# Small stores every two steps, and folds that run five gathers behind, in a graph kernel's gather stage

## What is computed

```python
hw = jnp.einsum('ni,rio->rno', h, weight)          # 8 relations + self
msg = hw[rel, src] + bias[rel]                     # one row of 128 floats per edge
agg = jax.ops.segment_max(msg, dst, num_segments=n)
...
msg = h_rel[etype, src]                            # layer 2, twice
agg = jax.ops.segment_sum(msg, dst, num_segments=h.shape[0])
...
agg = jax.ops.segment_sum(t[src] * norm, dst, ...) # layer 3, four times
```

## Time and profile before

| | us |
|---|---|
| median of 3 runs | 3251.54 (3245.12 to 3256.81) |
| the profiled execution | 3260.87 |
| its span, first to last instruction | 3259.1 |
| the stage's first and last gather (L823), starts | 279.9 and 1423.8 |
| POOL busy in the gathers L823 | 906.2 |
| DVE waiting for gathered data | 367.2 |

### The profile page before, as it was taken

The page is one execution under the profiler, slowest core; times in us unless marked ns, Lnnn a source line. Parts: engine busy times, 40 slices in busy tenths (PEclk is TensorE's granted clock), DMA queues, the critical chain, the costliest instruction groups (busy, mean ns, idle before and its releaser), DMA issues. The chain is left out here.

```text
span 3259.1 us, 35088 instructions
## 1 busy us (share of the span) xinstructions
PE 2356.9 (72%) x12626; PEld 1177.6 (36%) x12626; DVE 1342.1 (41%) x2638; ACT 863.4 (26%) x1563; POOL 979.7 (30%) x870
## 2 busy tenths in 40 slices
PE   0583555555555555554699999998999999659995
PEld 0121111111111111122445555554555555347773
DVE  2617666666666666654210000002000000247675
ACT  1233656566665565642200000000000000210000
POOL 1314777777777777760000000000000000000000
PEclk9976667765666676666899999998999999769997
DMA  2431444454444444433143333315333333120000
GB/s 69 162 131 70 175 167 173 166 183 159 172 166 168 172 160 168 158 142 135 58 176 139 141 142 141 141 61 189 139 129 140 139 141 121 65 77 1 2 1 22
DMA packets 98038, 412.25 MB, mean 126 GB/s; under 512 B 20059, under 2 KB 43680, under 8 KB 79020
## 3 DMA queue, kind: packets, MB, share of 16 engines
q1 hardware_dynamic: 55398, 343.29, 28.0%
q0 software_dynamic: 27312, 56.42, 5.8%
q10 hardware_dynamic: 15126, 9.99, 1.0%
HBM read 252.08 MB, written 163.93 MB: 128 GB/s over the span
## 5 line engine op out<-in xcount | busy, mean ns | idle before, releaser
L1410 PE MATMUL ps_out<-arena,cut 128*128 128x512 fp8e4 x4900 | 1074.5, 380 | 3.0 <-DVE cut L1053 3.0
L823 POOL DMA_INDIRECT arena<-table_rel,key_rel x784 | 906.2, 1156 | 294.3 <-issue 228.3
L879 PE MATMUL ps_out<-arena 128*128 128x400 f16 x1568 | 531.1, 465 | 502.3 <-DVE arena L852 408.3
L903 ACT ACTIVATE arena<-ps_out 128x800 fp8e4<-128x800 f32 x784 | 607.8, 836 | 423.3 <-PE ps_out L879 420.5
L1410 PEld LDWEIGHTS ps_out<-arena,cut 128*128 128x128 f16 x4900 | 479.7, 98 | 567.2 <-issue 5.2
L835 DVE SCALAR_TENSOR_TENSOR arena<-arena,keep_max 128x128 f32<-128x128 f32 x784 | 272.3, 347 | 374.0 <-DMA arena<-table_rel,key_rel 367.2
L879 PEld LDWEIGHTS ps_out<-arena 128*128 128x128 f16 x1568 | 122.6, 112 | 814.7 <-DVE arena L852 434.8
L1378 ACT ACTIVATE tT<-ps_t 128x128 f32<-128x128 f32 x50 | 13.8, 277 | 1121.9 <-PE ps_t L1400 1121.9
L1093 PE MATMUL ps_out<-arena,cut 128*128 128x384 fp8e4 (+1 forms) x1500 | 214.8, 305 | 81.1 <-DVE cut L1053 53.2
L1362 DVE TENSOR_SCALAR CS<-ps_out,unit 128x512 f32<-128x512 f32 x49 | 36.7, 748 | 491.1 <-PE ps_out L1410 491.1
L1362 DVE TENSOR_SCALAR CS<-ps_out 128x512 f32<-128x512 f32 x49 | 33.8, 691 | 493.1 <-PE ps_out L1410 493.1
(11 more groups left out here) (252 smaller groups left out, 1423.4 us busy)
## 6 DMA issues: line engine op xcount, KB each, us to landing
arena<-adjacency SPq DMA_DIRECT2D x98, 1600.0 KB, 6.7
adjacency<-arena SPq DMA_DIRECT2D x49, 1600.0 KB, 5.6
running_rows<-arena SPq DMA_DIRECT2D x56, 896.0 KB
arena<-adjacency_plain SPq DMA_DIRECT2D x50, 400.0 KB, 7.9
table_rel<-arena SPq DMA_DIRECT2D x25, 512.0 KB
arena<-table_rel,key_rel POOLq DMA_INDIRECT x784, 3.0
adjacency_plain<-adj SPq DMA_DIRECT2D x25, 400.0 KB, 6.7
edge_rows<-edge_dst ACTq DMA_DIRECT2D x1, 3125.5 KB
```

The source lines that it names most:

```text
L823: e.indirect_dma_start(message(t), None, table, bass.IndirectOffsetOnAxis(key[:, t:t + 1], 0)).then_inc(s_msg[t % both], 16)
L879: last = e.matmul(g.ps_out[:, u % 2, q * 512:q * 512 + KW], g.hot_low[:, b % 2, k, :, q], g.hot_spot[:, b % 2, k, :, q], start=True, stop= ...
L903: e.activation(g.half[h % 2].rearrange("p (a w x) -> p a w x", a=NT, x=R * WIN)[:, :, at:at + 2, :], g.ps_out[:, u % 2, 0:1024].rearrange( ...
L1410: last = e.matmul(g.ps_out[:, h, 0:512], g.cut[:, a, part, :], adj[:, a, :], start=a + part == 0, stop=a + part == NT)
```

## The change

It has two parts. The stores go out in pieces, at most one of each kind for every two steps: the running maxima two rows at a time (128 KB, 1 KB per partition), a half tile of the adjacency in five pieces (320 KB, 2560 bytes per partition) at steps 6, 8, 10, 12 and 14 behind its completion, a plain tile in three pieces (128, 128 and 144 KB) from 16 steps behind its completion on. And the fold of step t waits until `s_begun` stands at t + 6 instead of t + 3: the gather of step t + 5 is about to be issued, where before it was that of t + 2. The counts in the waits on the store semaphores follow the number of pieces. Nothing is changed in what POOL, PE and ACT issue, nor in the order of DVE's work.

```diff
@@ -55,6 +55,8 @@
+BEHIND = 6
+ROWS, PARTS, THIRDS = 2, 5, ((0, 1024), (1024, 2048), (2048, 3200))
@@ -827,9 +829,9 @@
             def step(t):
                 e.wait_ge(s_msg[t % both], 16 * (t // both + 1))
-                e.wait_ge(s_begun, min(t + 3, STEPS))
+                e.wait_ge(s_begun, min(t + BEHIND, STEPS))
                 if t % HALF == 0 and t >= both:
-                    e.wait_ge(s_out[t // HALF % 2], 16 * (t // both))
+                    e.wait_ge(s_out[t // HALF % 2], 16 * (HALF // ROWS) * (t // both))
@@ -888,7 +890,7 @@
                 if at == 0 and 2 <= m < NT - 1:
-                    e.wait_ge(s_one[m % 2], 16 * (m // 2))
+                    e.wait_ge(s_one[m % 2], 16 * len(THIRDS) * (m // 2))
@@ -898,7 +900,7 @@
                     if at == 0 and h >= 2:
-                        e.wait_ge(s_sto[h % 2], 16 * (h // 2))
+                        e.wait_ge(s_sto[h % 2], 16 * PARTS * (h // 2))
@@ -906,24 +908,32 @@
         @block.sync
         def _(e):
-            for t in range(1, STEPS + 1):
-                if t % HALF == 0:
-                    h = t // HALF - 1
+            for t in range(ROWS, STEPS + 3 * halfsteps, ROWS):
+                if t <= STEPS:
+                    h, at = (t - ROWS) // HALF % 2, (t - ROWS) % HALF
                     e.wait_ge(s_run, t)
-                    e.dma_start(running[:, h * HALF:(h + 1) * HALF, :], g.run[:, h % 2, :, :]).then_inc(s_out[h % 2], 16)
-                if t % halfsteps == 0:
-                    h = t // halfsteps - 1
-                    e.wait_ge(s_adj, t)
-                    e.dma_start(g.adjacency[h, :, :], g.half_u8(h % 2)).then_inc(s_sto[h % 2], 16)
-                if t % (2 * halfsteps) == 0 or t == STEPS:
-                    m = (t - 1) // (2 * halfsteps)
-                    e.wait_ge(s_plain, t // PAIRS)
-                    e.dma_start(g.adjacency1[m, :, :], plain(m).bitcast(U8)).then_inc(s_one[2 if m == NT - 1 else m % 2], 16)
+                    e.dma_start(running[:, t - ROWS:t, :], g.run[:, h, at:at + ROWS, :]).then_inc(s_out[h], 16)
+                h, part = (t - 6) // halfsteps - 1, (t - 6) % halfsteps // ROWS
+                if 0 <= h < HALVES and part < PARTS:
+                    lo, hi = (x * (NT // PARTS) * R * HD for x in (part, part + 1))
+                    if part == 0:
+                        e.wait_ge(s_adj, (h + 1) * halfsteps)
+                    e.dma_start(g.adjacency[h, :, lo:hi], g.half_u8(h % 2)[:, lo:hi]).then_inc(s_sto[h % 2], 16)
+                m, part = (t - halfsteps) // (2 * halfsteps) - 1, (t - halfsteps) % (2 * halfsteps) // ROWS
+                if 0 <= m < NT - 1 and part < len(THIRDS):
+                    lo, hi = THIRDS[part]
+                    if part == 0:
+                        e.wait_ge(s_plain, min((m + 1) * tilebatches, BATCHES))
+                    e.dma_start(g.adjacency1[m, :, lo:hi], plain(m)[:, lo:hi].bitcast(U8)).then_inc(
+                        s_one[m % 2], 16)
+            e.wait_ge(s_plain, BATCHES)
+            for lo, hi in THIRDS:
+                e.dma_start(g.adjacency1[NT - 1, :, lo:hi], plain(NT - 1)[:, lo:hi].bitcast(U8)).then_inc(s_one[2], 16)
```

More of the change, by code:

```diff
@@ L922, in _ @@
+            e.wait_ge(s_plain, BATCHES)
+            for lo, hi in THIRDS:
+                e.dma_start(g.adjacency1[NT - 1, :, lo:hi], plain(NT - 1)[:, lo:hi].bitcast(U8)).then_inc(s_one[2], 16)
             for h in range(2):
[L923 to L926, removed]
+                e.wait_ge(s_out[h], 16 * (HALF // ROWS) * (STEPS // both))
+                e.wait_ge(s_sto[h], 16 * PARTS * ((HALVES + 1 - h) // 2))
+                e.wait_ge(s_one[h], 16 * len(THIRDS) * (NT // 2))
@@ L927, in aggregate_and_build @@
+            e.wait_ge(s_one[2], 16 * len(THIRDS))
     join_chains(g, ALU.max)
```

## The result

The changed kernel takes 3142.44 us (median of 4 runs, 3132.68 to 3146.58) against 3248.73 us: a ratio of 0.9665, 95% interval 0.9634 to 0.9696. It is faster by about 106 us, where 160 were forecast; the forecast of 3090 misses the interval, and the measured time lies in the range of 3076 to 3150, near the price of rival 1 (3145), though not by that rival's cause.

A forecast was written before the change was run, and what follows sets the result against it. POOL's gathers were taken to bound the kernel, lengthened 166.1 us by DVE's instructions near their starts. Later folds -163 and the stage's end +1 gave -162 us: 3090 us against the median, range 3076 to 3150.

The forecast's parts named there:

- rival 1: DVE's folds: partly late behind two one-hots, or landings pass 6 us and DVE still catches up; 3145 us, chance 0.15.
- What bounds the kernel: Gathers on POOL pace the stage; badly placed DVE instructions lengthen them beyond 0.944 us each, 166.1 us together.
- Part (a): Fold's wait at t + 6: `s_begun` releases each fold 0.25 us ahead of a gather; gain 163 us of 166.1.
- Part (b): Stores in pieces: 712 issues instead of 130, 233 us more on SP, all hidden.
- Part (c): DMA engines' cost of pieces: 1.6 us of 2.5 per two steps; gathers land within 4.3 us.
- rival 2: DMA transfers become the bound, deciding from 0.13 us a packet on; 3285 us at 0.16, chance 0.05.
- Part (d): End of the stage: more store issues behind ACT's last product, taken as +1 us.
- Rival 3: Folds tied to a wrong place, 0.06 us ahead of gathers, so every gather loses twice; 3700 us, chance 0.04.
- rival 4: Gathers' lengthening is chance and the same with any timing, so nothing changes; 3251 us, chance 0.06.

The follow-up runs named there:

- e11: Kernel before, whole stores, with the fold waiting for `s_begun` at t + 20 and three unused-semaphore increments on DVE ahead of each fold: 3101.08 us, 0.9532.
- e3: Changed kernel with the fold waiting for `s_begun` at t + 18 instead of t + 6: 3127.83 us, 0.9645 of the kernel before.
- e1: Changed kernel with the old count t + 3 in the fold's wait, so the small stores alone: 3147.63 us, 0.9705 of the kernel before.
- e9: Changed kernel with the fold's wait at t + 18 and three unused-semaphore increments on DVE ahead of each fold: 3100.35 us, 0.954.

## Why the prediction came out as it did

**What bounds the kernel** held in full: POOL's gathers pace the stage, other engines' waits cost nothing, and the 166.1 us are due to DVE's instructions near a gather's start. e11, with whole stores, took back 157 us of the 166 by moving the folds alone, and its 3101 us are within 11 of the 3090 that had been forecast for the change. That the change's own time fell into the range is luck: the range reached up to 3150 for rival 1's sake, and the gain came from a part that the sum had at nothing.

**Part (a)** is where the forecast failed, in its first sentence. "That count is reached 5 periods and the head of one behind the start of gather t" took an increment ahead of a gather in the code for an event ahead of that gather in time. It is made when the sequencer gets there, 12 to 13 gathers early. The evidence I leaned on, five folds put down to POOL's sequencer, was coincidence: an increment comes some 0.02 us behind the end of a gather, and a fold whose data land at about that moment is put down to it. The trace tells the two apart. The five folds started 0.03 to 0.05 us behind an increment, while the 540 of e3 that really waited for one started 0.105 behind it in the median; and of the one fold of the five whose landing is in the trace, at 1358.5, the start is 0.02 behind its own data, as with every fold that data released. That also gives the 0.07 us by which e3 missed. What should have warned me stood in the earlier trace rows: five releases out of 784 by a wait that, by my own working (2.25 us, less than the shortest landing of 2.4), should have been met first always. A look at the first and last start of the increments' own line, beside the gathers', would have settled it. The term: 163 us taken, 111.6 measured, and these were part (b)'s, not (a)'s.

**Part (b)** was costed at nothing beyond its issues, and it was nearly the whole gain: alone (e1) it took the lengthening from 166.1 to 803.0 - 740.1 = 62.9 us. I had read that landings behind whole stores set the folds' places, and then gave the cure to the wait. With the wait idle, the pieces made late landings rare (over 3.5 us: 29 of 308 instead of 81 of 224), and DVE stayed nearer to the quiet pattern of the earlier trace rows. A change whose parts overlap in what they cure should be costed with each part failing; "the wait does nothing, the stores do what they can" was missing among the rivals.

**Part (c)**: landings of 4.3 us or sooner were forecast, 5.5 measured; the load of the DMA engines came out right (1.6 us in 2.5 per two steps, measured 0.573 x 2.64 = 1.5). A mean packet of q1 took 0.06 us, between the 0.04 and 0.10 taken for the two kinds of pieces and far from the 0.13 from which rival 2 would have decided. Once folds are tied to gathers, 712 stores and 130 take the same time (e9 0.954, e11 0.9532). The Trainium skill's rule in "DMA: Bandwidth & Descriptors", "Rules for kernel authors", which is against small transfers, is not borne out here: the cost of each of the 582 more stores stayed hidden.

**Part (d)**: +1 us was forecast for the end; from the last gather to the first of `join_chains` it is 1324.85 - 1309.60 = 15.2 us against 1441.37 - 1423.81 = 17.6, so -2.3. The eight issues took 5 us and not 2.9, and from ACT's last product to `join_chains` it is 7.9 us against 7.4, so the stores' own share was +0.5. The rest came from ahead of them: ACT ended its last product 7.3 us behind the start of the last gather instead of 10.1 (1316.94 and 1433.94).

**Rivals.** Rival 1's price fits (43 to 83 us lost, 54.6 measured) and half of its text, "DVE still catches up"; but not since landings pass 6 us, and not by the fold behind two one-hots: of the 55 us, only 11 are of gathers at whose start a fold was the instruction in the way, whichever fold, and the others were behind one-hots. Rival 3, the wrong place, was half right in kind: e3 tied nearly every fold to a place 0.07 us off and lost 38 us. Its cliff was not reached in a run that decides. Rival 2 fell with the packet above, rival 4 with e3, e9 and e11, where only the timing differs. (The 0.217 us per gather in rivals 1 and 3 should be 166.1 / 784 = 0.212; no price moves by more than 2 us for it.) The Trainium skill's "SBUF — State Buffer", section "Who interferes with whom", has a DVE instruction with two inputs in SBUF contend with a GpSimd instruction that reads SBUF. The rows agree in kind: a DVE instruction with two inputs in SBUF that is running at a certain moment of the gather holds it up; that it is the port is not shown. But the gather's start is not that moment. In e3 the fold outlasts the start by 0.17 us and costs 0.05, which puts the moment at some 0.12 behind the start.

## What to carry to other kernels

A semaphore raised by a queue just ahead of an operation tells that the sequencer has come there, not that the engine has; compare the first and last times of the two lines before building a wait on it. Where two engines contend for something short at a fixed point of a periodic operation, where the other's work falls can matter more than how much it is: fix the place by tying it to an event of the pacing engine, and measure it in tens of nanoseconds. And when a stall comes from late data, giving the consumer more lag can do what smaller transfers do.

## What was not expected of the hardware

- POOL's sequencer was 15.5 us, about 12 gathers, ahead of the executing gather at the end of the changed kernel, and 16.9 us in the kernel before.
- A fold that starts 0.05 us behind a gather's start costs it nothing (0.944 us, e9), one 0.18 us ahead 0.05 us (e3), a one-hot 0.11 us ahead 0.47 us (1.41, changed kernel at 629), and a fold 0.06 us ahead 0.79 us.
- Three increments on DVE's sequencer moved the start of a released fold by 0.23 us, from 0.18 ahead to 0.05 behind; a fold that waited for an increment started 0.105 us after it (e3), one that waited for data 0.02 us after the landing.
- One chip of those used ran the kernel before in 3461.57 us instead of 3250, and even the ratios of variants were others there. That stays open.
